# A graph network on one core: rounds of 13 groups, two tiles of each round fetched row by row, node relus on VectorE

## The chip, the cores and the metric

The kernel runs on one core of a Trainium2 chip. The metric is the device time of one execution in microseconds (us). The kernel before takes 6143.23 us (median of 3 runs, 6143.08 to 6143.71).

## What is computed

A three-layer message-passing network over 12,500 nodes and 212,500 edges, all in float32 with 128 features. `x`, the indices and the weights are inputs; the edges come sorted by destination.

```python
h = relu(layernorm(x))                      # 12500 x 128
h = h @ enc_w + enc_b;  h_list = [h]
for l in range(3):
    e   = edge_attr @ edge_w[l] + edge_b[l]            # 212500 x 16 -> x 128
    msg = relu(h_list[l][src] + e)                     # rows gathered by source node
    agg = segment_sum(msg, dst)                        # summed by destination node
    z   = (1 + eps[l]) * h_list[l] + agg
    z   = relu(z @ w1[l] + b1[l]) @ w2[l] + b2[l]      # 128 -> 256 -> 128
    h_list.append(relu(z))
out = x + concat(h_list) @ out_w + out_b
```

## The kernel before, in words

Edges are cut into tiles of 128 (one edge for each partition) and tiles into groups of four: 416 groups in a layer, the last of one tile. A ring of 16 slots in the SBUF tensor `rows` holds the gathered source rows, one slot for a group; a *round* is one turn of the ring, 26 rounds in a layer. The three layers run one after the other, since the rows that a layer gathers are the ones that the layer before stored.

For every group k of a round b the engines do this, each in its own program order:

- **GpSimd** (line 399) waits until the slot's last user is summed (`agg_done`, line 423) and issues one indirect DMA for each tile, which gathers 128 rows of 512 bytes. In slots 13 (`SHARED_GROUP`) and 14 (`SYNC_GROUP`) it gathers three tiles only; the fourth tile is fetched row by row, with one small DMA for each row, by other engines.
- **SyncE** (`fetch_body`, lines 339 to 349) fetches all 128 rows of the fourth tile of slot 14 and rows 0 to 47 of that of slot 13: 176 DMAs in a round (line 336). The addresses come from `row_at`, loaded into registers in chunks of 16 (line 333).
- **ScalarE** fetches rows 48 to 127 of slot 13's fourth tile, eight after each of its first ten relus of a round (`fetch_rows`, lines 568 to 574).
- **TensorE** makes the edge terms of group k + 2 (`edge_terms`, line 669), then the window sums of group k (`window_sums`, line 673), which wait for the relu of group k (line 735).
- **VectorE** builds the one-hot matrix of group k (line 914), adds the window sums of group k - 2 to the aggregate (`accumulate`, line 924; it waits for TensorE), and then adds the edge terms of group k to the gathered rows (`add_terms`, line 928), once rows and edge terms are there. At the end of a round it adds the last two window sums before it starts the next.
- **ScalarE** applies the relu to the group's rows (line 584), which releases TensorE's sums. Its program is one stream: wait for the sum of group k, relu of group k, then whatever else stands behind group k in `edge_body`: the load of the next edge attributes (line 564, behind the second group of a half), node work, and the row fetches.

So VectorE's add of group k needs the window sums of group k - 2, and these need the relu of group k - 2.

Node work is done in *units* of 512 nodes (24 in a layer and a rest of 256) inside the rounds. A round has two halves of 8 groups; a table worked out in the prologue says which unit, if any, each half carries. In the second, third and fourth group of a half TensorE runs `node_z` (lines 692, 694), `node_h` (line 700) and `node_out` (lines 710, 713). ScalarE runs `relu_z` in the third (line 526, two instructions) and `relu_h` in the fourth (line 535). VectorE runs `node_take` in the fifth (lines 965 to 971), and ScalarE stores the unit's rows in the sixth.

A prologue of some 130 us normalises x, encodes it, stores the table of layer 0 from SyncE (line 298) and prepares the indices. GpSimd's gathers of layer 0 start while its second part still runs on TensorE, ScalarE and VectorE.

Of the kernel before, what the change touches and what calls it, by code (L numbers as in the profile page):

```python
# [5 lines left out]
P = 128  # L6
# [5 lines left out]
HB = 8  # L12
RING = 16
# [8 lines left out]
SYNC_GROUP, SHARED_GROUP = 14, 13  # L22
SHARED_BY_SYNC = 48
CHUNK = 16
ACT_ROWS = 8
# [4 lines left out]
def gnn_kernel(nc, x_t, src_t, src_g, dst_t, dst_g, ea_t, enc_w, enc_b, edge_w, edge_b, w1, b1, w2, b2,  # L30
# [17 lines left out]
    NB = NGP // HB  # L48
    NBU = NG // HB
# [7 lines left out]
    assert ND * UT + LAST == -(-nodes // P) and NB == -(-NG // HB) and NGP <= P * GR and NI <= NBU  # L57
    assert REST == RING and EP % CHUNK == 0 and SHARED_BY_SYNC % CHUNK == 0
    assert (EP - SHARED_BY_SYNC) % ACT_ROWS == 0 and (EP - SHARED_BY_SYNC) // ACT_ROWS < SHARED_GROUP < SYNC_GROUP < RING - 1

# [7 lines left out]
    with ctx:  # L68
# [11 lines left out]
        rows = sb("rows", [P, RING, TG, D])  # L80
# [179 lines left out]
        def uses_of_half(half):  # L260
            return NFULL + (REST > half * HB)

# [20 lines left out]
        def _(sp):  # L283
            for part in range(2):
                load_x(sp, part)
            sp.wait_ge(s_zeroed, 4)
            sp.dma_start(attr[0][0:KA - 1, :], ea_t[:, 0:HB * EP]).then_inc(attr_in[0], 16)
            for j in range(TG):
                cols = slice(j * D, (j + 1) * D)
                sp.dma_start(edgew[j * KE:(j + 1) * KE, :, cols], edge_w.rearrange("l k n -> k l n"))\  # L290
                  .then_inc(s_edgew, 16)
                sp.dma_start(edgew[KA - 1:KA, :, cols], edge_b.rearrange("(a l) n -> a l n", a=1))\
                  .then_inc(s_edgew, 16)
            for i in range(NI):
                sp.wait_ge(p_biased, i + 1)
                made = p_rows[i % 4].rearrange("p t d -> p (t d)")
                if i < ND:
                    sp.dma_start(h_units[0][:, i, :], made).then_inc(p_stored[i % 4], 16)
                else:
                    sp.dma_start(h_last[0], made[:, 0:LAST * D]).then_inc(p_stored[i % 4], 16)  # L300
                if i == 8:
                    sp.dma_start(dst_n, dst_g.rearrange("c (g e) -> c g e", g=GR)).then_inc(s_dst, 16)
                if i == 10:
                    sp.dma_start(dst_i, dst_t).then_inc(s_dst_t, 16)
                if i == 12:
                    sp.dma_start(idx[0:EP, :], src_t).then_inc(idx_in, 16)
                    for u, k in enumerate((SYNC_GROUP, SHARED_GROUP)):
                        of_group = src_g.rearrange("(b t) e -> b t e", t=RING * TG)[:, k * TG + TG - 1, :]
                        sp.dma_start(row_at[u:u + 1, :].rearrange("a (b e) -> a b e", e=EP), of_group.unsqueeze(0))\
                          .then_inc(row_at_in, 16)  # L310
                if i == 14:
                    sp.dma_start(encb[:, :], enc_b).then_inc(s_par, 16)
                    sp.dma_start(b1s[:, :], b1).then_inc(s_par, 16)
                    sp.dma_start(b2s[:, :], b2).then_inc(s_par, 16)
                if i == 16:
                    sp.dma_start(eps1[:, 0:L], eps.partition_broadcast(P)).then_inc(s_par, 16)
                    sp.dma_start(outw[:, :, :], out_w.rearrange("(l k) n -> k l n", k=D)).then_inc(s_par, 16)
                    sp.dma_start(outb[:, :], out_b.partition_broadcast(P)).then_inc(s_par, 16)

            named = itertools.count()  # L320
            for l in range(L):
# [7 lines left out]
                def fetch_rows(b, u, group, count, fetched):  # L329
                    for first in range(0, count, CHUNK):  # L330
                        with ExitStack() as held:
                            at = [held.enter_context(sp.register(f"sync_at{next(named)}")) for _ in range(CHUNK)]
                            sp.load(at, row_at[u:u + 1, bass.ds(b * EP + first, CHUNK)])  # L333
                            for i in range(CHUNK):
                                row = rows[first + i:first + i + 1, group, TG - 1, :]
                                sp.dma_start(row.bitcast(u8), table_row(l, sp, at[i])).then_inc(fetched, 16)  # L336
# [23 lines left out]
                fetch_body(NFULL)  # L360
# [7 lines left out]
        def _(g):  # L368
# [34 lines left out]
            for l in range(L):  # L403
# [12 lines left out]
                for group in range(NG):  # L416
# [3 lines left out]
                    if l == 0 and group == HB:  # L420
                        g.wait_ge(s_ready, 1)
# [12 lines left out]
        def _(act):  # L434
            for s in (hid_ready, h_ready):
                act.sem_inc(s, N0)
# [82 lines left out]
            for l in range(L):  # L519
                load_weights(l)  # L520

                def relu_z(i, cols=UC):
                    n = i + l * NU
                    for c, ps in enumerate((zh_ps, zt_ps)):
                        wait_apart(act, z_done, n * HC + (c + 1 + N0))
                        nc.scalar.activation(hid[:, c, 0:cols], ps[:, 0:cols], ACT.Relu,  # L526
                                             bias=b1s[:, l * HC + c:l * HC + c + 1])\
                          .then_inc(hid_ready, 1)

                def relu_h(i, cols=UC):  # L530
                    n = i + l * NU
                    act.wait_ge(h_done, n + (1 + N0))
                    act.wait_ge(o_done, n + N0)
                    wait_apart(act, seeded, (L - 1) * NU + N0 if l == L - 1 else n + N0)
                    nc.scalar.activation(h_t[:, 0:cols], zh_ps[:, 0:cols], ACT.Relu, bias=b2s[:, l:l + 1])\  # L535
                      .then_inc(h_ready, 1)

# [16 lines left out]
                def node_body(i):  # L554
                    relu_z(i)
                    relu_h(i)
                    (store if l < L - 1 else store_out)(i)

                def load_next_attr(b, half):
# [3 lines left out]
                    else:  # L563
                        act.dma_start(attr[1 - half][0:KA - 1, :],
                                      ea_t[:, bass.ds((b * 2 + half + 1) * (HB * EP), HB * EP)])\
# [10 lines left out]
                def edge_body(b, groups):  # L576
                    for k in range(groups):
                        half, kk = k // HB, k % HB
                        if kk == 0 and groups - k >= HB:
# [22 lines left out]
                nodes_left(act, first, node_body)  # L602
                relu_z(ND, LAST * P)
                relu_h(ND, LAST * P)
# [5 lines left out]
        def _(pe):  # L610
# [67 lines left out]
            for l in range(L):  # L678
# [45 lines left out]
                def edge_body(b, groups):  # L724
                    first_group = b * RING + l * NG

                    def e_terms(k):
                        half, kk = k // HB, k % HB
# [11 lines left out]
                    for k in range(groups):  # L740
                        half, kk = k // HB, k % HB
                        if kk == 0 and groups - k >= HB:
# [4 lines left out]
                        if kk in (1, 2, 3) and groups - half * HB >= HB:  # L747
                            with pe.If(unit > 0):
                                if kk == 1:
                                    wait_apart(pe, added, first_group + (half * HB + S0))  # L750
# [21 lines left out]
        def _(dve):  # L772
            dve.sem_inc(summed, S0)
            dve.sem_inc(added, S0)
            for s in (seeded, rows_ready, o_added):
# [50 lines left out]
            def find_units():  # L826
# [7 lines left out]
                own(v.tensor_reduce(later_lo[cur][:, 0:NB], base_row[:, :].rearrange("a (b g) -> a b g", g=HB), AX.X,  # L834
                                    ALU.min))
# [121 lines left out]
            for l in range(L):  # L957
                dve.wait_ge(seeded, l * NU + N0)

                def node_take(i, tiles=UT):  # L960
# [13 lines left out]
                def edge_body(b, groups):  # L974
# [8 lines left out]
                    for k in range(groups):  # L983
                        half, kk = k // HB, k % HB
                        if kk == 0:
                            if groups - k >= HB:
                                unit = load_unit(dve, b * 2 + half)
                            dve.load(bases[half * HB:(half + 1) * HB], base_row[0:1, bass.ds(b * RING + half * HB, HB)])
# [4 lines left out]
                        by_rows = {SYNC_GROUP: sync_fetched, SHARED_GROUP: shared_fetched}  # L993
# [5 lines left out]
                        dve.wait_ge(gathered[k], (b + (l * uses_of_slot(k) + 1)) * (16 * (TG - (k in by_rows))))  # L999
# [12 lines left out]
                nodes_left(dve, first, node_take)  # L1012
# [63 lines left out]
```

## Time and profile before

| | us |
|---|---|
| median of the runs | 6143.23 |
| the profiled execution | 6140.5 |
| its span, first to last instruction | 6138.7 |
| GpSimd busy | 4595.5 (75%) |
| TensorE busy (matmul) | 4785.9 (78%) |
| VectorE busy | 1656.2 (27%) |
| ScalarE busy | 985.9 (16%) |
| mean granted TensorE clock | 0.581 of 2.4 GHz |

Busy time counts the engines' data instructions. Loads into registers and the issuing of DMAs take time on an engine's sequencer and count as idle there, so SyncE is not in the table at all, though it issues 13,728 row DMAs, and ScalarE, which issues 6,240, looks idler than it is. In the timeline such work stands under `SPq` and `ACTq`. A gather on GpSimd is a row `DMA_INDIRECT`; the idle time in brackets behind it is the time since the one before.

### The profile page before, as it was taken

How to read it: one execution, taken by the hardware profiler on the slowest of the kernel's cores; microseconds unless marked ns; L12 is line 12 of the kernel's file. 1: busy time of each engine (PE TensorE's matmuls, PEld its weight loads, DVE VectorE, ACT ScalarE, POOL GpSimd, SP SyncE). 2: the span in 40 equal slices, each digit the busy share in tenths (PEclk: the TensorE clock that was granted, in tenths of full speed). 3: DMA queues.
4: the chain of work that ended last, by engine and by line, in shares of the span. 5: the costliest groups of instructions: out<-in, count | busy, mean ns of one | idle time of the engine just before them, and what ended most of it. 6: DMA issues, size and time to landing. Idle time of an engine off the chain costs nothing.

```text
span 6138.7 us, 99522 instructions
## 1 busy us (share of the span) xinstructions
PE 4785.9 (78%) x14396; PEld 2978.1 (49%) x14397; DVE 1656.2 (27%) x4182; ACT 985.9 (16%) x1583; POOL 4595.5 (75%) x4920
## 2 busy tenths in 40 slices
PE   7877777777777777777777778777777777777777
PEld 5544444444444444444444444444444444444444
DVE  6222222222222222222222222222222222222222
ACT  4111111111111111111111111111111111111111
POOL 6777777777777677777777777767777777777776
PEclk8555555555555555555555555555555555555555
DMA  4222222222222222222222222222222222222222
GB/s 141 65 65 65 65 65 65 65 65 63 65 65 65 64 64 64 66 65 66 66 66 66 64 66 66 66 63 64 65 65 65 63 65 65 65 65 64 65 65 60
DMA packets 226648, 409.09 MB, mean 67 GB/s; under 512 B 102529, under 2 KB 125444, under 8 KB 225460
## 3 DMA queue, kind: packets, MB, share of 16 engines
q0 software_dynamic: 154464, 316.65, 19.8%
q10 hardware_dynamic: 38032, 69.39, 3.9%
q1 hardware_dynamic: 33579, 18.23, 1.0%
q14 instruction: 557, 4.55, 0.2%
q8 instruction: 16, 0.26, 0.0%
HBM read 378.17 MB, written 25.69 MB: 66 GB/s over the span
## 4 chain that ended last, share of the span: by engine, by line
POOL 32%; PE 17%; issue 16%; SPq 15%; DMA 11%; DVE 4%; ACT 3%; ACTq 1%; DVEq 0%; POOLq 0%
POOL rows L399 32%; SPq L336 12%; DMA rows<-h_table,idx 11%; PE bank L673 11%; PE bank L669 5%; SPq L333 3%; DVE rows L928 3%; ACT rows L584 3%; ACTq L574 1%; PE bank L692 0%; PE bank L647 0%; PE bank L694 0%; PE bank L639 0%; PE bank L632 0%; DVE onehot L790 0%
## 5 line engine op out<-in xcount | busy, mean ns | idle before, releaser
L399 POOL DMA_INDIRECT rows<-h_table,idx x4827 | 4558.6, 944 | 1505.4 <-issue 1335.1
L673 PEld LDWEIGHTS bank<-onehot,rows 128*128 128x128 f32 x9966 | 2066.9, 304 | 2718.0 <-ACT rows L584 2607.6
L673 PE MATMUL bank<-onehot,rows 128*128 128x64 f32 x9966 | 2212.9, 397 | 1300.8 <-ACT rows L584 1295.4
L669 PE MATMUL bank<-edgew,attr 65*128 65x512 f32 x2496 | 2216.2, 1000 | 9.3 <-DMA w2s<-w 9.3
L928 DVE TENSOR_TENSOR rows<-bank,rows 128x512 f32<-128x512 f32 x1248 | 860.9, 690 | 3470.0 <-DMA rows<-h_table,idx 3128.0
L584 ACT ACTIVATE rows<-rows 128x512 f32<-128x512 f32 x1248 | 783.5, 628 | 5048.0 <-DVE rows L928 4837.8
L669 PEld LDWEIGHTS bank<-edgew,attr 65*128 65x128 f32 x2496 | 657.9, 307 | 269.3 <-issue 269.3
L914 DVE TENSOR_TENSOR onehot<-bank,dst_rel 128x256 f32<-128x256 f32 x1248 | 518.7, 416 | 204.7 <-issue 204.7
L924 DVE TENSOR_TENSOR agg_t<-bank,agg_t 128x64 f32 x1248 | 271.7, 218 | 696.5 <-PE bank L673 691.5
L692 PE MATMUL bank<-agg_t,w1s 128*128 (+1 forms) x150 | 149.1, 1097 | 1.5 <-DVE agg_t L924 1.5
L713 PE MATMUL bank<-outw,h_t 128*128 128x128 f32 x588 | 149.2, 397 | 0.7 <-ACT h_t L535 0.7
L700 PE MATMUL bank<-hid,w2s 128*128 128x512 f32 x300 | 145.2, 607 | 0.0
L713 PEld LDWEIGHTS bank<-outw,h_t 128*128 128x128 f32 x588 | 141.9, 325 | 1.4 <-ACT h_t L535 1.4
L694 PE MATMUL bank<-agg_t,w1s 128*128 (+1 forms) x150 | 127.8, 952 | 0.0
L526 ACT ACTIVATE hid<-bank,b1s 128x512 f32<-128x512 f32 (+1 forms) x150 | 94.5, 667 | 22.7 <-PE bank L694 12.2
L694 PEld LDWEIGHTS bank<-agg_t,w1s 128*128 128x128 f32 x150 | 50.4, 336 | 74.9 <-issue 74.4
L700 PEld LDWEIGHTS bank<-hid,w2s 128*128 128x128 f32 x300 | 52.2, 196 | 37.1 <-issue 34.4
L971 DVE TENSOR_TENSOR out_acc<-bank,out_acc 128x512 f32 (+1 forms) x75 | 50.5, 674 | 18.0 <-PE bank L713 18.0
L535 ACT ACTIVATE h_t<-bank,b2s 128x512 f32<-128x512 f32 (+1 forms) x75 | 49.8, 664 | 22.8 <-PE bank L700 22.4
L394 POOL TENSOR_SCALAR rows<-out_acc,rstd,nmr 128x128 f32<-128x128 f32 x75 | 32.3, 448 | 23.4 <-DVE nmr L806 23.4
L965 DVE COPY h_n<-bank 128x512 f32<-128x512 f32 (+1 forms) x50 | 33.7, 674 | 59.1 <-PE bank L710 59.1
L647 PEld LDWEIGHTS bank<-outw,hid 128*128 128x128 f32 x200 | 28.9, 210 | 27.9 <-issue 20.8
(83 smaller groups left out, 468.4 us busy)
## 6 DMA issues: line engine op xcount, KB each, us to landing
rows<-h_table SPq DMA_DIRECT2D x13728, 0.5 KB
rows<-h_table ACTq DMA_DIRECT2D x6240, 0.5 KB
rows<-h_table,idx POOLq DMA_INDIRECT x4827, 2.5
attr<-ea_t ACTq DMA_DIRECT2D x155, 256.0 KB
h_table<-h_n ACTq DMA_DIRECT2D x48, 256.0 KB, 2.3
h_table<-rows SPq DMA_DIRECT2D x24, 256.0 KB, 2.7
out<-out_acc ACTq DMA_DIRECT2D x24, 256.0 KB, 2.3
out_acc<-x_t ACTq DMA_DIRECT2D x4, 1280.0 KB, 16.3
```

The costliest lines, as they stand in the source:

```text
L333: sp.load(at, row_at[u:u + 1, bass.ds(b * EP + first, CHUNK)])
L336: sp.dma_start(row.bitcast(u8), table_row(l, sp, at[i])).then_inc(fetched, 16)
L399: return g.indirect_dma_start(dst, None, h_table[l % 2], bass.IndirectOffsetOnAxis(ap=index, axis=0))
L584: nc.scalar.activation(part, part, ACT.Relu).then_inc(relued, 1)
L669: return nc.tensor.matmul(dst[0:EP, 0:tiles * D], cols, edgew[:, l, 0:tiles * D], start=True, stop=True)
L673: last = nc.tensor.matmul(dst[:, 0:WIN], rows[0:EP, slot, j, :], onehot[0:EP, hot_slot, j, :], start=(j == 0), stop=(j == tiles - 1))
L694: nc.tensor.matmul(zt_ps[:, 0:cols], w1s[:, D:2 * D], moving, start=True, stop=True).then_inc(z_done, 1)
L700: last = nc.tensor.matmul(zh_ps[:, 0:cols], w2s[:, c, :], hid[:, c, 0:cols], start=(c == 0), stop=(c == HC - 1))
L713: last = nc.tensor.matmul(zh_ps[:, j * D:(j + 1) * D], cols[:, j, :], outw[:, l + 1, :], start=True, stop=True)
L914: return v.tensor_tensor(onehot[0:EP, slot, 0:tiles, :], numbers[0:EP, :].unsqueeze(1).broadcast_to([EP, tiles, WIN]), dst_rel[0:EP, bass. ...
L924: return v.tensor_tensor(cols, ps[:, 0:WIN], cols, ALU.add)
L928: return v.tensor_tensor(part, ps[0:EP, 0:tiles * D].rearrange("p (t d) -> p t d", d=D), part, ALU.add)
```

## The change

- A round has 13 groups instead of 16 (`RING`), and a layer 32 rounds instead of 26. `rows` keeps its 16 slots (`SLOTS`) for the prologue's use, but the ring turns over 13 of them.
- The halves of a round have 7 and 6 groups.
- The slots whose fourth tile is fetched by rows are 10 and 11. In the last round of a layer nothing is fetched by rows; GpSimd gathers all four tiles there.
- SyncE fetches 128 + 16 rows in a round instead of 128 + 48, with register loads of 32 addresses instead of 16.
- ScalarE fetches 112 rows in a round instead of 80: 28 rows at a time (`ACT_ROWS`), behind groups 0, 2, 4 and 6 (`ACT_EVERY`), instead of 8 rows behind each of groups 0 to 9.
- `relu_z` and `relu_h` of the nodes run on VectorE (as `tensor_scalar` with add and max), in the third and fourth group of a half, in front of `node_take` in the fifth.
- In the prologue the loads of the first edge attributes and of the edge weights, which stood ahead of SyncE's first store, stand behind stores 18 and 19 to 22 of 25.

The core of the diff:

```diff
-HB = 8
-RING = 16
+HALVES = ((0, 7), (7, 6))
+HB = 7
+RING = 13
+SLOTS = 16
-SYNC_GROUP, SHARED_GROUP = 14, 13
-SHARED_BY_SYNC = 48
-CHUNK = 16
-ACT_ROWS = 8
+SYNC_GROUP, SHARED_GROUP = 11, 10
+SHARED_BY_SYNC = 16
+CHUNK = 32
+ACT_ROWS = 28
+ACT_EVERY = 2
@@ SyncE, prologue
-            sp.wait_ge(s_zeroed, 4)
-            sp.dma_start(attr[0][0:KA - 1, :], ea_t[:, 0:HB * EP]).then_inc(attr_in[0], 16)
...
+                if i == 18:
+                    sp.wait_ge(s_zeroed, 4)
+                    sp.dma_start(attr[0][0:KA - 1, :], ea_t[:, 0:HB * EP]).then_inc(attr_in[0], 16)
+                if 0 <= i - (NI - TG - 2) < TG:
+                    j = i - (NI - TG - 2)
+                    cols = slice(j * D, (j + 1) * D)
+                    sp.dma_start(edgew[j * KE:(j + 1) * KE, :, cols], edge_w.rearrange("l k n -> k l n"))\
+                      .then_inc(s_edgew, 16)
...
@@ SyncE, layers
-                fetch_body(NFULL)
@@ GpSimd
-                    if slot in (SYNC_GROUP, SHARED_GROUP):
+                    if slot in (SYNC_GROUP, SHARED_GROUP) and group < NFULL * RING:
                         tiles = TG - 1
@@ ScalarE, edge_body: behind the relu of group k
-                        if kk in (2, 3, 5) and groups - half * HB >= HB:
+                        if kk == 5:
                             with act.If(unit > 0):
-                                (relu_z if kk == 2 else relu_h if kk == 3 else
-                                 store if l < L - 1 else store_out)(unit_before(unit))
-                        if k == 0 and not (isinstance(b, int) and b == 0 and l == 0):
-                            wait_apart(act, agg_done, b * RING + (l * NG + SHARED_GROUP + 1 + S0 - RING))
-                        if k < (EP - SHARED_BY_SYNC) // ACT_ROWS:
-                            fetch_rows(b, SHARED_BY_SYNC + k * ACT_ROWS)
+                                (store if l < L - 1 else store_out)(unit_before(unit))
+                        if not isinstance(b, int):
+                            if k == 0:
+                                wait_apart(act, agg_done, b * RING + (l * NG + SHARED_GROUP + 1 + S0 - RING))
+                            if k % ACT_EVERY == 0 and k // ACT_EVERY < (EP - SHARED_BY_SYNC) // ACT_ROWS:
+                                fetch_rows(b, SHARED_BY_SYNC + k // ACT_EVERY * ACT_ROWS)
@@ VectorE
+                def relu_z(i, cols=UC):
+                    n = l * NU + i
+                    for c, ps in enumerate((zh_ps, zt_ps)):
+                        dve.wait_ge(z_done, n * HC + (c + 1 + N0))
+                        v.tensor_scalar(hid[:, c, 0:cols], ps[:, 0:cols], b1s[:, l * HC + c:l * HC + c + 1], 0.0,
+                                        ALU.add, ALU.max).then_inc(hid_ready, 1)
@@ VectorE, edge_body: behind add_terms of group k
-                        if kk == 4 and groups - half * HB >= HB:
+                        if kk in (2, 3, 4):
                             with dve.If(unit > 0):
-                                node_take(unit_before(unit))
+                                (relu_z, relu_h, node_take)[kk - 2](unit_before(unit))
```

## Rows read from the trace of the kernel before

**Rows 1.** The page's head: span, and busy time of each engine.
```profile
span 6138.7 us, 99522 instructions
PE 4785.9 (78%) x14396; PEld 2978.1 (49%) x14397; DVE 1656.2 (27%) x4182; ACT 985.9 (16%) x1583; POOL 4595.5 (75%) x4920
```
**Rows 2.** The gathers' line: count, duration (min/median/max ns), first and last start.
```profile
L399 POOL DMA_INDIRECT rows<-h_table,idx x4827: 940/944/3425, 66.8 to 6124.1; - x194
```
**Rows 3.** The view of waits: who waited for whom, us, times, longest.
```profile
POOL rows L399 <- PE bank L673: 164.6, 539, 0.3
...
DVE rows L928 <- DMA rows<-h_table: 237.2, 25, 16.9
```
**Rows 4.** Timeline of ScalarE, layer 0's first round: start, duration, what, idle before.
```profile
132.98 0.63 ACT L584 ACTIVATE rows<-rows 128x512 f32<-128x512 f32 x1 [5.99 <-DVE rows L928]
...
149.47 0.63 ACT L584 ACTIVATE rows<-rows 128x512 f32<-128x512 f32 x1 [3.16 <-DVE rows L928]
150.38 2.68 ACTq L574 DMA_DIRECT2D rows<-h_table  x8
153.17 0.63 ACT L584 ACTIVATE rows<-rows 128x512 f32<-128x512 f32 x1 [3.06 <-DVE rows L928]
...
160.86 0.63 ACT L584 ACTIVATE rows<-rows 128x512 f32<-128x512 f32 x1 [3.27 <-DVE rows L928]
...
165.34 0.63 ACT L584 ACTIVATE rows<-rows 128x512 f32<-128x512 f32 x1 [3.85 <-DVE rows L928]
```
**Rows 5.** The same timeline further on, groups 10 to 15 and the next round's first.
```profile
173.22 1.15 ACT L584 ACTIVATE rows<-rows 128x512 f32<-128x512 f32 x2 [3.80 <-DVE rows L928]
176.91 0.63 ACT L584 ACTIVATE rows<-rows 128x512 f32<-128x512 f32 x1 [2.54 <-DVE rows L928]
180.56 0.63 ACT L584 ACTIVATE rows<-rows 128x512 f32<-128x512 f32 x1 [3.02 <-DVE rows L928]
183.89 0.63 ACT L584 ACTIVATE rows<-rows 128x512 f32<-128x512 f32 x1 [2.70 <-DVE rows L928]
187.15 0.63 ACT L584 ACTIVATE rows<-rows 128x512 f32<-128x512 f32 x1 [2.63 <-DVE rows L928]
193.04 0.63 ACT L584 ACTIVATE rows<-rows 128x512 f32<-128x512 f32 x1 [5.25 <-DVE rows L928]
```
**Rows 6.** Timeline of SyncE's queue, around the register load between two chunks.
```profile
3006.08 1.87 SPq L336 DMA_DIRECT2D rows<-h_table  x2
3007.68 5.03 SPq L336 DMA_DIRECT2D rows<-h_table  x16
```
**Rows 7.** Engines' busy time in two stretches, with the granted clock as PEclk.
```profile
core 0: us, PE busy (x) PEld busy (x) DVE busy (x) ACT busy (x) POOL busy (x), PEclk, DMA share, GB/s
147.00:225.00 78.00, 75.86 (x209) 46.95 (x208) 25.61 (x63) 12.98 (x21) 58.79 (x64) 0.50 0.24 61
2600.00:2677.40 77.40, 60.21 (x181) 36.92 (x181) 20.26 (x51) 11.80 (x19) 58.50 (x63) 0.59 0.25 65
```
**Rows 8.** Timeline of TensorE where a node unit's first matmuls stand.
```profile
303.10 2.02 PE L669 MATMUL bank<-edgew,attr 65*128 65x512 f32 x2
...
306.63 2.02 PE L692 MATMUL bank<-agg_t,w1s 128*128 x2
...
310.52 1.00 PE L673 MATMUL bank<-onehot,rows 128*128 128x64 f32 x8
```
**Rows 9.** Timeline across the seam from layer 0 to layer 1.
```profile
2078.76 0.94 POOL L399 DMA_INDIRECT rows<-h_table,idx  x1 [0.30 <-issue]
...
2082.51 0.31 ACT L584 ACTIVATE rows<-rows 128x128 f32<-128x128 f32 x1 [1.00 <-DVE rows L928]
...
2092.60 0.94 POOL L399 DMA_INDIRECT rows<-h_table,idx  x1 [12.89 <-issue]
...
2099.63 0.63 ACT L584 ACTIVATE rows<-rows 128x512 f32<-128x512 f32 x1 [11.01 <-DVE rows L928]
```
**Rows 10.** Timeline at the end: the last relu on edge rows.
```profile
6128.09 0.31 ACT L584 ACTIVATE rows<-rows 128x128 f32<-128x128 f32 x1 [0.82 <-DVE rows L928]
```
**Rows 11.** VectorE's scaling from SBUF to SBUF in `node_take`: count, duration, first and last.
```profile
L967 DVE TENSOR_SCALAR agg_t<-h_t,eps x50: 344/477/683, 240.6 to 4113.2; 128x512 f32 x48, 128x256 f32<-128x256 f32 x2
```

More of the change, by code:

```diff
@@ L47, in gnn_kernel @@
     NGP = NTE // TG
-    NB = NGP // HB
-    NBU = NG // HB
+    NB = NGP // RING * 2
+    NBU = NB
     L = w1.shape[0]
@@ L79, in gnn_kernel @@
         agg_t = sb("agg_t", [P, NP + WIN])
-        rows = sb("rows", [P, RING, TG, D])
+        rows = sb("rows", [P, SLOTS, TG, D])
         attr = [sb(f"attr{i}", [KA, HB * EP]) for i in range(2)]
@@ L260, in uses_of_half, with in_half @@
         def uses_of_half(half):
-            return NFULL + (REST > half * HB)
+            return NFULL + (REST > HALVES[half][0])
+        def in_half(k):
+            half = int(k >= HALVES[1][0])
+            return half, k - HALVES[half][0]
         def load_left(eng):
@@ L330, in fetch_rows @@
                     for first in range(0, count, CHUNK):
+                        here = min(CHUNK, count - first)
                         with ExitStack() as held:
-                            at = [held.enter_context(sp.register(f"sync_at{next(named)}")) for _ in range(CHUNK)]
-                            sp.load(at, row_at[u:u + 1, bass.ds(b * EP + first, CHUNK)])
-                            for i in range(CHUNK):
+                            at = [held.enter_context(sp.register(f"sync_at{next(named)}")) for _ in range(here)]
+                            sp.load(at, row_at[u:u + 1, bass.ds(b * EP + first, here)])
+                            for i in range(here):
                                 row = rows[first + i:first + i + 1, group, TG - 1, :]
@@ L419, in _ @@
                         g.wait_ge(idx_in, 16)
-                    if l == 0 and group == HB:
+                    if l == 0 and group == 8:
                         g.wait_ge(s_ready, 1)
@@ L520, in _ @@
                 load_weights(l)
[L522 to L536, printed above, removed]
                 def store_out(i):
@@ L563, in load_next_attr @@
                     else:
-                        act.dma_start(attr[1 - half][0:KA - 1, :],
-                                      ea_t[:, bass.ds((b * 2 + half + 1) * (HB * EP), HB * EP)])\
+                        start, n = HALVES[1 - half]
+                        cols = bass.ds((b + half) * (RING * EP) + start * EP, n * EP)
+                        act.dma_start(attr[1 - half][0:KA - 1, 0:n * EP], ea_t[:, cols])\
                            .then_inc(attr_in[1 - half], 16)
@@ L577, in edge_body @@
                     for k in range(groups):
-                        half, kk = k // HB, k % HB
-                        if kk == 0 and groups - k >= HB:
+                        half, kk = in_half(k)
+                        if kk == 5:
                             unit = load_unit(act, b * 2 + half)
@@ L601, in _ @@
                 far_passes(act, n_far, far_pass)
-                nodes_left(act, first, node_body)
-                relu_z(ND, LAST * P)
-                relu_h(ND, LAST * P)
+                nodes_left(act, first, store if l < L - 1 else store_out)
                 if l < L - 1:
@@ L727, in e_terms @@
                     def e_terms(k):
-                        half, kk = k // HB, k % HB
+                        half, kk = in_half(k)
                         if kk == 0:
@@ L740, in edge_body @@
                     for k in range(groups):
-                        half, kk = k // HB, k % HB
-                        if kk == 0 and groups - k >= HB:
+                        half, kk = in_half(k)
+                        if kk == 0:
                             unit = load_unit(pe, b * 2 + half)
@@ L746, in edge_body @@
                         sums(k)
-                        if kk in (1, 2, 3) and groups - half * HB >= HB:
+                        if kk in (1, 2, 3):
                             with pe.If(unit > 0):
                                 if kk == 1:
-                                    wait_apart(pe, added, first_group + (half * HB + S0))
+                                    wait_apart(pe, added, first_group + (HALVES[half][0] + S0))
                                     node_z(unit_before(unit))
@@ L774, in _ @@
             dve.sem_inc(added, S0)
-            for s in (seeded, rows_ready, o_added):
+            for s in (seeded, rows_ready, o_added, hid_ready, h_ready):
                 dve.sem_inc(s, N0)
@@ L833, in find_units @@
                 cur = 0
-                own(v.tensor_reduce(later_lo[cur][:, 0:NB], base_row[:, :].rearrange("a (b g) -> a b g", g=HB), AX.X,
-                                    ALU.min))
+                in_rounds = base_row[:, :].rearrange("a (b r) -> a b r", r=RING)
+                low = later_lo[cur][:, 0:NB].rearrange("a (b h) -> a b h", h=2)
+                for half, (start, n) in enumerate(HALVES):
+                    own(v.tensor_reduce(low[:, :, half], in_rounds[:, :, start:start + n], AX.X, ALU.min))
                 reach = 1
@@ L958, in _, with relu_h, node_body @@
                 dve.wait_ge(seeded, l * NU + N0)
+                def relu_z(i, cols=UC):
[4 more added lines that the diff above has]
+                                        ALU.add, ALU.max).then_inc(hid_ready, 1)
+                def relu_h(i, cols=UC):
+                    n = l * NU + i
+                    dve.wait_ge(h_done, n + (1 + N0))
+                    dve.wait_ge(o_done, n + N0)
+                    dve.wait_ge(seeded, (L - 1) * NU + N0 if l == L - 1 else n + N0)
+                    v.tensor_scalar(h_t[:, 0:cols], zh_ps[:, 0:cols], b2s[:, l:l + 1], 0.0, ALU.add, ALU.max)\
+                     .then_inc(h_ready, 1)
+                def node_body(i):
+                    relu_z(i)
+                    relu_h(i)
+                    node_take(i)
                 def node_take(i, tiles=UT):
@@ L983, in edge_body @@
                     for k in range(groups):
-                        half, kk = k // HB, k % HB
+                        half, kk = in_half(k)
                         if kk == 0:
-                            if groups - k >= HB:
-                                unit = load_unit(dve, b * 2 + half)
-                            dve.load(bases[half * HB:(half + 1) * HB], base_row[0:1, bass.ds(b * RING + half * HB, HB)])
+                            unit = load_unit(dve, b * 2 + half)
+                            dve.load(bases[k:k + HALVES[half][1]], base_row[0:1, bass.ds(b * RING + k, HALVES[half][1])])
                         tiles = real_tiles(b, k)
```

33 lines of the change are left out of this document (14 added, 19 removed).

## The prediction

> **What bounds the kernel now.** I read the page's busy times first [rows 1], then the line of the costliest group, the gathers [rows 2], then the waits. Busy shares mislead here: GpSimd shows 75%, but it issued 4827 gathers from 66.8 to 6124.1 us. Take off the two seams between layers (the first one keeps it idle from 2078.76 to 2092.60 [rows 9], the second some 2 us longer) and a gather is left every 1.25 us for the whole span. Its waits for a free slot were never longer than 0.3 us [rows 3], which is the ordinary space between two gathers. So GpSimd sets the pace: 62 gathers in a round, 77.5 us. TensorE comes second: 60.2 busy us in 77.4 [rows 7]. The reader should see two things beside this. First, nobody else's chain is far away: in layer 0, where the first relu on edges comes only at 132.98 us [rows 4] while the gathers have run since 66.8, the rest of the engines work off a backlog, and that stretch shows what their chain can do when the data is there. Second, ScalarE's 16% hides its DMA issues.
>
> **The gathers.** Two by-row tiles in 31 rounds instead of 26 make 62 instead of 52 tiles a layer that GpSimd doesn't gather, so 30 gathers fewer over three layers: 30 x 1.25 = 37.5 us off, if GpSimd still sets the pace. A round of 13 groups is then 50 gathers, 62.5 us. That is the time every other chain has to meet.
>
> **SyncE.** 16 rows in a chunk take 5.03 us, and from the row at 3006.08 with one more behind the load to the end there were 1.87 us [rows 6]: about 0.32 us a row and 1.3 us for a load of 16 addresses. After: 144 x 0.32 = 46 us and five loads of, I take it, 1.5 to 2.3 us, 54 to 58 us in a round of 62.5. It had 176 x 0.32 + 11 x 1.3 = 71 of 77.5. It keeps up in both, though its 128 rows must follow the sums of group 11 one round before; I give it no price.
>
> **ScalarE, the term that decides.** [rows 4] have the backlogged pace with 8 rows behind each relu: from a relu to the first row 0.91 us (the address load is in it), 2.68 us for the 8 rows, 0.11 to the next relu; 3.70 from relu to relu (149.47 to 153.17). That hid under the 5.0 us which four gathers take. Now 28 rows stand behind one relu. Rows: 28 x 0.32 = 9.0 us (9.7 at the 0.34 of the eight). Load and rest: no row has 28 addresses; between 1.0 (the load doesn't grow) and 2.3 (it grows per address as fast as it may from 8 to 16); I take 2.1, since the loads of 16 in [rows 6] are longer than those of 8 in [rows 4]. So 11.1 us a burst, bounds 9.9 and 12.2. In it the relu of the next, odd group can't run: two groups cost 11.1 + about 0.7, where their eight gathers bring 10.0. From the relu of group 0 to that of group 7 there are four bursts (44.4), three steps of about 0.75 to an even group (0.54 in [rows 5], more with the attribute load), and the unit number's load before group 5, 0.8 (160.86 to 165.34 against 3.7 without it [rows 4]): 47.4 us. On arrival alone it would be 35.
>
> Then the round isn't over. From group 7's relu on, the chain is the one of [rows 5]: two relus together behind the last burst (173.22), then 176.91, 180.56, 183.89, 187.15, and 193.04 for the first of the next round. TensorE paces it: edge terms and sums of a group take about 3.4 us, VectorE's add of group k waits for the sums of k - 2, and at the round's end VectorE must add the last window before it starts again. Seven relus in, five groups and the boundary on, is just what groups 7 to 12 and the next group 0 are after the change: 19.8 us. Together 67.2 us for a round, against 62.5 from GpSimd. TensorE can't work ahead during the bursts, as its sums wait for the relus that are stuck.
>
> **Nodes.** With 512 nodes a unit and 30 nodes a group, 14 units of a layer fall into second halves of the first 31 rounds, 9 into first halves, one into the last round. In a second half the unit's 8 us of TensorE work lie in the TensorE-paced part; but behind it the array runs at its upper level (a group's sums in 1.00 us, after edge terms at 2.02 us for two before it [rows 8]), which gives some back; and VectorE, not ScalarE, now waits for the z products. I take 4.5 us, between 3 and 8. In a first half there are 5 idle us of TensorE in each pair of groups: 1.3 us, between 0 and 3. A round: (14 x 4.5 + 9 x 1.3) / 31 = 2.4. ScalarE loses 225 relus of about 0.65 us, which I credit at nothing beyond this, as the bursts are what holds it.
>
> So **a round takes 69.6 us** and the chain ScalarE, TensorE, VectorE sets the pace in all 93 of them; GpSimd waits for slots instead.
>
> **The ring of 13.** With less lead GpSimd would stall in layer 0's start: 50 gathers from 66.8 end at about 132, and the first slot is free after the first sums, some 3 us behind the relu at 132.98: 4 us on GpSimd. It costs nothing where GpSimd isn't the bound.
>
> **The prologue.** The moved loads leave the first input loads alone and meet SyncE among its last stores; nine issues of about 0.6 us against a 60 us lead of the gathers over the first relu. Nothing, give or take 2 us; if the x tiles come sooner, a microsecond gained.
>
> **The sum.** First relu at 132.98 [rows 4]. 93 rounds x 69.6 = 6473. Three last rounds without bursts at 3.4 us a group and one unit: 3 x 45.5 = 136.5. Two seams from the last relu to the first gather (2082.51 to 2092.60 [rows 9]), 2 x 10.1, and from there to the relu (2099.63), 2 x 7.0. The end: 6138.7 - 6128.09 = 10.6 [rows 1, 10]. Span 6787. The profiled execution was 4.5 us of span below the median of the runs: **6792 us**, 10.6% slower.
>
> The bounds on the term that decides: with bursts of 9.9 and units at their lowest a round is 42.6 + 19.8 + 1.4 = 63.8, and the time 6253; with bursts of 12.2 and units at their highest 51.8 + 19.8 + 4.5 = 76.1 and 7397. I put the likely part of this, 6270 to 7150, as the range of the case.
>
> **A rule that speaks against this chain.** [rows 7] show TensorE busy 75.9 of 78 us at a granted clock of 0.50, the lower level of 1.2 GHz; only behind the node matmuls of [rows 8] is it at 2.4 GHz. I take TensorE's pace from these rows. The Trainium skill (TensorE: Matmul & The Clock Gate, Part 1) says that the clock gate opens after sustained activity; by it a TensorE that is backlogged would run near the upper level, and [rows 7] disagree.
>
> **Rivals.** *GpSimd stays the bound.* The chain from group 7 on is faster than [rows 5] (TensorE at the upper level, about 2 us a group, which makes the 19.8 some 14), or bursts overlap with relus in a way I don't see. Then 6143.2 - 37.5 + 4 for the shorter ring = 6110. For it: the total of ScalarE's work, 4 x 11.1 + 13 x 0.7 = 54 us, does fit in 62.5; against it: it isn't spread, and [rows 4, 5] are the same instructions in the same order. 12%. *Just at the edge*, a round of 62.5 to 63: 6150, 3%. *GpSimd is the bound but is held up by VectorE.* 225 node relus come to VectorE at about 0.68 us. If each kept a gather from being issued, up to 153 us: 6110 + 153 = 6263. Against it: VectorE's scaling from SBUF to SBUF, 50 times [rows 11], left gathers at 1.25 us. The Trainium skill (SBUF — State Buffer, Who interferes with whom) says that VectorE in a two-port mode and GpSimd shut each other out for a whole instruction; [rows 11] don't show it as a cost. The decisive point is whether GpSimd's rows near such relus show more than 0.3 us between gathers. 3%. *SyncE becomes the bound*: 58 us plus the landing and the sums of group 11, near 62.5; it decides only if a round were under 63, so it is inside the first rival.
>
> **Chances.** The forecast's chain 82%, GpSimd bound 12%, edge 3%, lock-out 3%. 0.2% is about what a measurement of this kernel can tell from no change. Faster 0.13, same 0.02, slower 0.85. The range 6270 to 7150 leaves out the first rival and the tails.
>
> **What would show it.** Right: GpSimd's waits for TensorE's sums (line 399 behind `window_sums`) rise from 165 us to hundreds, in all three layers; ScalarE's timeline has `ACTq` blocks of 28 rows of about 9 us with one relu, then two relus together; relu of group 0 to group 7 about 47 us, to the next group 0 about 67 to 75. VectorE's wait for row DMAs falls away. Wrong: gathers at 1.25 us without a stall past layer 0's first round, or relus between the rows of a block; or bursts under 9.9 us.

## The result, and the profile after

The changed kernel takes 6851.86 us (median of 4 runs, 6846.06 to 6853.34), the kernel before beside it 6143.47: a ratio of 1.115, 95% interval 1.113 to 1.117. The prediction was 6792 us in a range of 6270 to 7150, slower.

The page's head and the two lines of its chain of work that ended last (shares of the span by engine, then by line):

```profile
span 6844.3 us, 106750 instructions
PE 4772.2 (70%) x14396; PEld 3103.4 (45%) x14397; DVE 1846.6 (27%) x4408; ACT 828.4 (12%) x1358; POOL 4567.8 (67%) x4890
...
ACTq 51%; PE 26%; issue 15%; DVEq 3%; DVE 3%; ACT 2%; DMA 0%; POOL 0%; SPq 0%
ACTq L561 41%; PE bank L658 13%; ACTq L558 8%; PE bank L654 8%; ACT rows L571 2%; DVEq L994 2%; DVE rows L915 1%; PE bank L698 1%; PE bank L685 1%; PE bank L677 1%; ACTq L251 1%; PE bank L679 1%; ACTq L552 1%; DVEq L251 1%; PE bank L632 0%
```

ScalarE's busy time fell to 828 us, against 986 in [rows 1], and yet half of the chain is now on its queue: line 561 issues the single rows, line 558 loads their addresses. GpSimd is out of it. The same line of the page before had GpSimd (POOL) at a third:

```profile
POOL 32%; PE 17%; issue 16%; SPq 15%; DMA 11%; DVE 4%; ACT 3%; ACTq 1%; DVEq 0%; POOLq 0%
```

The waits after say the same (who waited for whom, us, times, longest):

```profile
ACT rows L571 <- issue: 3826.7, 417, 11.8
DVE agg_t L911 <- PE bank L658: 3562.8, 982, 10.5
...
POOL rows L408 <- PE bank L658: 758.8, 392, 6.8
```

The last line answers to the first of [rows 3]: GpSimd waits up to 6.8 us for a slot where it never waited over 0.3, 759 us in all against 165. Its 4797 gathers still stand 1.25 us apart when nothing holds them. "issue" in the first line is ScalarE's own issuing: its relus wait for the engine itself.

One round of the changed kernel on ScalarE's timeline (start, duration, what, idle before):

```profile
3017.62 0.63 ACT L571 ACTIVATE rows<-rows 128x512 f32<-128x512 f32 x1 [6.20 <-DVE rows L915]
3019.72 8.97 ACTq L561 DMA_DIRECT2D rows<-h_table  x28
3028.80 0.63 ACT L571 ACTIVATE rows<-rows 128x512 f32<-128x512 f32 x1 [10.54 <-issue]
...
3029.55 0.63 ACT L571 ACTIVATE rows<-rows 128x512 f32<-128x512 f32 x1
3031.73 9.06 ACTq L561 DMA_DIRECT2D rows<-h_table  x28
3040.90 1.15 ACT L571 ACTIVATE rows<-rows 128x512 f32<-128x512 f32 x2 [10.72 <-issue]
3043.08 8.95 ACTq L561 DMA_DIRECT2D rows<-h_table  x28
3052.98 1.15 ACT L571 ACTIVATE rows<-rows 128x512 f32<-128x512 f32 x2 [10.93 <-issue]
3055.19 9.03 ACTq L561 DMA_DIRECT2D rows<-h_table  x28
3064.33 0.63 ACT L571 ACTIVATE rows<-rows 128x512 f32<-128x512 f32 x1 [10.21 <-issue]
...
3089.79 0.63 ACT L571 ACTIVATE rows<-rows 128x512 f32<-128x512 f32 x1 [6.25 <-DVE rows L915]
```

Four blocks of 28 rows, 9 us each, with two relus behind each of the first three; 46.7 us from the relu of group 0 to that of group 7, and 25.5 more to the next group 0 at 3089.79 (this round has a node unit in its second half).

From the start times of all relus on edge rows (line 571) I worked out how long the rounds take, in 93 rounds: 24 without a node unit 68.1 us, 39 with one in the second half 72.7, 30 with one in the first half 69.1; **70.3 us in the mean**, against the 77.5 that GpSimd's 62 gathers take for 16 groups before. That is 5.41 us a group, and 4.84 before.

GpSimd's stall sets in late, because its lead has to be used up first. In layer 1 the relu of a round's first group stood 0, 7, 18, 25, 31, 37, 48 and 53 us later, from round to round, than the arrival of its rows allowed; from there on it stayed at 52 to 61 us, near the 62.5 us that gathers for a full ring of 13 take. Layer 2 did the same, a little later. In layer 0 it is there from the start.

### The profile page after: what moved, and what is told of

Same layout as the page of the kernel before. It is cut to its first block, busy times and chain, and to the rows that moved or that the text cites. A ratio compares the mean times of both kernels' runs of the same rounds, so it can differ in the third digit from the quotient of the medians.

```text
span 6844.3 us, 106750 instructions
## 1 busy us (share of the span) xinstructions
PE 4772.2 (70%) x14396; PEld 3103.4 (45%) x14397; DVE 1846.6 (27%) x4408; ACT 828.4 (12%) x1358; POOL 4567.8 (67%) x4890
## 4 chain that ended last, share of the span: by engine, by line
ACTq 51%; PE 26%; issue 15%; DVEq 3%; DVE 3%; ACT 2%; DMA 0%; POOL 0%; SPq 0%
ACTq L561 41%; PE bank L658 13%; ACTq L558 8%; PE bank L654 8%; ACT rows L571 2%; DVEq L994 2%; DVE rows L915 1%; PE bank L698 1%; PE bank L685 1%; PE bank L677 1%; ACTq L251 1%; PE bank L679 1%; ACTq L552 1%; DVEq L251 1%; PE bank L632 0%
## 5 line engine op out<-in xcount | busy, mean ns | idle before, releaser
L658 PEld LDWEIGHTS bank<-onehot,rows 128*128 128x128 f32 x9966 | 2157.2, 310 | 3257.9 <-ACT rows L571 2695.3
L658 PE MATMUL bank<-onehot,rows 128*128 128x64 f32 x9966 | 2169.4, 394 | 2018.2 <-ACT rows L571 2015.0
L654 PE MATMUL bank<-edgew,attr 65*128 65x512 f32 x2496 | 2320.3, 1047 | 8.5 <-DMA w2s<-w 8.5
L571 ACT ACTIVATE rows<-rows 128x512 f32<-128x512 f32 x1248 | 757.0, 625 | 5950.0 <-issue 3826.7
L654 PEld LDWEIGHTS bank<-edgew,attr 65*128 65x128 f32 x2496 | 692.5, 321 | 307.5 <-issue 307.5
L951 DVE TENSOR_SCALAR hid<-bank,b1s 128x512 f32<-128x512 f32 (+1 forms) x150 | 110.7, 740 | 593.4 <-PE bank L677 537.0
L959 DVE TENSOR_SCALAR h_t<-bank,b2s 128x512 f32<-128x512 f32 (+1 forms) x75 | 55.5, 740 | 156.0 <-PE bank L685 156.0
```

What stands on the lines that cost most here:

```text
L571: nc.scalar.activation(part, part, ACT.Relu).then_inc(relued, 1)
L654: return nc.tensor.matmul(dst[0:EP, 0:tiles * D], cols, edgew[:, l, 0:tiles * D], start=True, stop=True)
L658: last = nc.tensor.matmul(dst[:, 0:WIN], rows[0:EP, slot, j, :], onehot[0:EP, hot_slot, j, :], start=(j == 0), stop=(j == tiles - 1))
```

## The experiments

All kernels are edits of the changed kernel. Ratios are to the kernel before, run in between on the same chip.

**The bursts.** If the row fetches on ScalarE's queue and what TensorE has left behind them set the round, two bursts fewer must give the time back, with the ring of 13 and the relus on VectorE still there. This kernel leaves out 56 of the 128 rows of the shared tile, so it computes something else; its time is what counts here.

```diff
+ACT_BURSTS = 2
...
-                            if k % ACT_EVERY == 0 and k // ACT_EVERY < (EP - SHARED_BY_SYNC) // ACT_ROWS:
+                            if k % ACT_EVERY == 0 and k // ACT_EVERY < ACT_BURSTS:
...
+                own(v.memset(rows[:, SHARED_GROUP, TG - 1, :], 0.0))
...
-                            take(dve, by_rows[k], 16 * EP)
+                            take(dve, by_rows[k], 16 * (EP if k == SYNC_GROUP else SHARED_BY_SYNC + ACT_BURSTS * ACT_ROWS))
```

> The changed kernel with two bursts of 28 row fetches on ScalarE instead of four; 56 rows of the shared tile are left out (what stands in those partitions of the buffer is used instead), everything else stays: ring of 13, node relus on VectorE, 50 gathers a round. Theory (ScalarE's bursts and TensorE behind them set a round): group 0 to 3 takes 24 us, from there to the next group 0 about 34 us, 58 and some 2 for nodes, under the 62.5 us of the gathers; GpSimd is the bound again at 1.25 us a gather: 6100 to 6140 us. Rival 'the ring of 13 starves GpSimd': stays near 6850. Rival 'VectorE's node relus': at least 6650.

Measured first: 9330 us, and 9367 for the kernel before beside it. This was on a chip on which the queues of SyncE and ScalarE issue slowly; it is told further down. The four kernels timed there say nothing on the theories, and each was timed on another chip too.

> The same kernel as e_2bursts, again, because in that call every kernel, the one before too, took 8.4 to 9.4 ms, with 0.7 us between many of SyncE's instructions. If SyncE issues a row every 0.32 us again: theory (bursts, then TensorE) 58 us of chain and 2 of nodes under the gathers' 62.5, so 6100 to 6140 us; the ring of 13 or VectorE's relus as the cause would leave it near 6850 or 6650. 56 rows of the shared tile are left out.

Measured: **6114.45 us**, ratio 0.996 (0.994 to 0.997). The waits:

```profile
POOL rows L409 <- issue: 1412.5, 4626, 0.3
POOL rows L409 <- PE bank L659: 64.5, 168, 7.0
```

GpSimd is the bound again. The median is 25 us below the kernel before beside it (6139.68), where 30 gathers fewer would give 37.5. In the profiled run a gather stood 1.2514 us behind the one before, against 1.2489, which makes 12 us over all of them; it isn't VectorE's relus, as the gathers took 944 ns in the median in the kernel with three bursts, which has them too, and 947 in the first run of the one with the relus on ScalarE. The shorter ring cost three stalls of 4.1, 6.7 and 2.5 us in layer 0's start, and none after. A round took 62.2 us in the mean.

Three bursts, with the same edit and `ACT_BURSTS = 3` (28 rows are left out):

> The changed kernel with three bursts of 28 rows instead of four; 28 rows of the shared tile are left out. Theory: group 0 to group 5 takes 35.9 us, from there 28 us to the next group 0, with nodes 66 us a round; 304 us outside the rounds: 6440 us, between 6380 and 6500. Not proportional to the bursts: the fourth costs 400 us, the third some 330, the second nothing. Rivals (ring, VectorE's relus): near 6850.

On the slow chip: 9115 us, before 9367. Again:

> The same kernel as e_3bursts (three bursts of 28 rows, 28 rows of the shared tile left out), with rows at 0.32 us again. Theory: group 0 to group 5 36.0 us, from there 0.54 + 3.15 + 3.4 + 3.4 + 3.4 + 3.3 + 3.3 + 6.8 = 27.3 to the next group 0, 63.3 us and 2.3 for nodes, 65.6 a round; 304 + 93 x 65.6 = 6405 us, between 6350 and 6450. If the time followed the number of rows, halfway between two bursts (6114) and four (6852): 6480.

Measured: **6388.54 us**, ratio 1.040 (1.038 to 1.041). A round took 65.6 us, the 65.6 that had been worked out. Two, three and four bursts give 62.2, 65.6 and 70.3 us: with two a round is the gathers' own, the third costs 3.4, the fourth 4.7. Only what goes beyond GpSimd's 62.5 us shows. In proportion to the rows it would have been 6480 us; the measured time stands 16 us below the 6405 of the forecast.

**The size of a burst or their sum.** The same 112 rows, spread:

```diff
-ACT_ROWS = 28
-ACT_EVERY = 2
+ACT_ROWS = 16
+ACT_EVERY = 1
```

> The changed kernel with the same 112 rows on ScalarE, as 16 rows behind each of groups 0 to 6 instead of 28 behind 0, 2, 4 and 6. Theory 'ScalarE's total before group 7 counts': 7 x 6.8 us + 1.5 us for the attribute and unit loads = 49 us, then 20 us: a round near 70 to 71, 6850 to 6930 us. Rival 'the size of a burst counts' (TensorE works between smaller bursts, so that nothing is left to catch up): below 6300.

On the slow chip: 8421 us, before 9367. Again:

> The same kernel as e_16x7, again. With rows at 0.32 us: theory 'ScalarE's total ahead of group 7 counts' 70 to 71 us a round, 6850 to 6930 us; rival 'the size of a burst counts' below 6300.

Measured: **7030.86 us**, ratio 1.145 (1.143 to 1.147), 100 us above the upper end of what was expected, and slower than 28 at a time. ScalarE's timeline:

```profile
3031.89 0.63 ACT L571 ACTIVATE rows<-rows 128x512 f32<-128x512 f32 x1 [6.98 <-issue]
3033.26 5.17 ACTq L561 DMA_DIRECT2D rows<-h_table  x16
3038.55 0.63 ACT L571 ACTIVATE rows<-rows 128x512 f32<-128x512 f32 x1 [6.03 <-issue]
```

6.7 to 6.8 us a step, and 7.6 at the two with another load beside it; 49 to 50 us to group 7, then the same 21: 70.1 us in a round without a unit, 72.4 in the mean. The sum ahead of group 7 counts, not its pieces; and smaller pieces have more address loads (1.4 us from relu to first row, seven times, against 2.1 four times). What the expectation missed are the units' 2.3 us a round, which it left out of its 70 to 71.

**The node relus.** Back on ScalarE, at their old places (`relu_z` and `relu_h` move with them; the unit's number is loaded at a half's first group instead of its sixth):

```diff
@@ ScalarE
-                        if kk == 5:
+                        if kk == 0:
                             unit = load_unit(act, b * 2 + half)
...
-                        if kk == 5:
+                        if kk in (2, 3, 5):
                             with act.If(unit > 0):
-                                (store if l < L - 1 else store_out)(unit_before(unit))
+                                (relu_z if kk == 2 else relu_h if kk == 3 else
+                                 store if l < L - 1 else store_out)(unit_before(unit))
@@ VectorE
-                        if kk in (2, 3, 4):
+                        if kk == 4:
                             with dve.If(unit > 0):
-                                (relu_z, relu_h, node_take)[kk - 2](unit_before(unit))
+                                node_take(unit_before(unit))
```

> The changed kernel with the node relus back on ScalarE, where they were before. Theory: they stand in the bursts' part of first halves and cost 2 us more there, and about the same in second halves: 6850 to 6950 us. Rival 'VectorE's relus, which make it wait for TensorE, are the cost': down to about 6650 us.

On the slow chip: 9438 us, before 9367. Again:

> The same kernel as e_act_relus (node relus back on ScalarE), with rows at 0.32 us again. Theory: 2 us more in rounds with a unit in the first half, the same in the others: 6850 to 6950 us. Rival 'VectorE's relus are the cost': down to about 6650 us.

Measured: **7079.54 us**, ratio 1.152 (1.151 to 1.154): worse than with them on VectorE, by 228 us, and 130 us above the range. The timeline of a round with a unit in its first half:

```profile
3033.87 0.63 ACT L592 ACTIVATE rows<-rows 128x512 f32<-128x512 f32 x1 [10.58 <-issue]
...
3034.66 0.63 ACT L592 ACTIVATE rows<-rows 128x512 f32<-128x512 f32 x1 [0.16 <-issue]
3038.47 0.69 ACT L533 ACTIVATE hid<-bank,b1s 128x512 f32<-128x512 f32 x1 [3.18 <-PE bank L701]
3040.18 0.69 ACT L533 ACTIVATE hid<-bank,b1s 128x512 f32<-128x512 f32 x1 [1.02 <-PE bank L703]
3042.26 9.43 ACTq L582 DMA_DIRECT2D rows<-h_table  x28
```

Group 1's relu was held until 3033.87 by the burst ahead, so TensorE's z products come only after it, and ScalarE stands at `relu_z` with its next burst behind it: 5 us lost. Rounds with a unit in the first half took 75.0 us, 6.0 more than with the relus on VectorE; those with one in the second half 73.1 against 72.7, those without 68.5 against 68.1. Over 93 rounds this is the 207 us between the two profiled spans. So this part of the change is worth some 200 to 230 us beside the bursts. Taking 225 relus off ScalarE had been credited at nothing, which was right for the 0.65 us of each and would have been wrong for their waits.

**The prologue.** The loads at their old place:

> The changed kernel with the loads of the first edge attributes and edge weights at their old place, ahead of SyncE's first store. Both theories: within 0.2% of the changed kernel's 6852 us; the first relu on edges at 133 to 135 us as in both traces.

The edit puts the load of `attr[0]` and the eight of `edgew` ahead of SyncE's first store again. Measured, in one run: 6842.65 us, 0.13% under 6851.86 and 3.4 us under the profiled run of the changed kernel. The first relu came at 137.6 us, outside the 133 to 135 expected, against 134.8; the last rounds made up for it (42.2 us in the mean, against 43.0), and a round took 70.28 us, against 70.32. So this part moves the first relu by 3 us and the whole by nothing that one run can show.

**A version that could keep GpSimd the bound.** All rows fetched, 100 of them on ScalarE, ten at a time:

```diff
-SHARED_BY_SYNC = 16
+SHARED_BY_SYNC = 28
...
-ACT_ROWS = 28
-ACT_EVERY = 2
+ACT_ROWS = 10
+ACT_EVERY = 1
```

> The changed kernel with 100 rows on ScalarE, 10 behind each of groups 0 to 9, and 28 + 128 on SyncE: all rows are fetched. Theory: a step with 10 rows is about 4.5 us (3.8 with 8, 6.8 with 16), under the 5.0 us of four gathers, and only three groups are left behind the last one: 45 + 2.5 + 0.5 + 3.2 + 6.8 = 58 us; SyncE needs 56 + 12 x 0.36 = 60 us. Both are under the gathers' 62.5: GpSimd is the bound, 6105 to 6135 us, 0.2 to 0.6% under the kernel before. Rival 'no margin is left' (SyncE's 60 us and the wait for its rows, or units on top): 6200 or more.

Measured: **6923.13 us**, ratio 1.127 (1.125 to 1.128). The 6105 to 6135 expected are badly missed, and the timeline shows where:

```profile
3031.89 0.63 ACT L571 ACTIVATE rows<-rows 128x512 f32<-128x512 f32 x1 [6.33 <-issue]
3033.23 3.33 ACTq L561 DMA_DIRECT2D rows<-h_table  x10
3036.67 0.63 ACT L571 ACTIVATE rows<-rows 128x512 f32<-128x512 f32 x1 [4.15 <-issue]
3039.29 3.31 ACTq L561 DMA_DIRECT2D rows<-h_table  x10
...
3073.22 3.45 ACTq L561 DMA_DIRECT2D rows<-h_table  x10
3079.58 0.63 ACT L571 ACTIVATE rows<-rows 128x512 f32<-128x512 f32 x1 [8.29 <-DVE rows L915]
```

From a relu to the first row it is 1.34 us at one step and 2.62 at the next, in turn. The trace's records of the address load have 1.0 to 1.4 us for the loads that begin at index 28, 48, 68, 88 and 108, and 2.2 to 2.6 us for 38, 58, 78, 98 and 118. These are loads of the same size in the same run, so where a load begins is what differs. The other part is the end: group 10 needs its last rows, which are issued just ahead of it (8.1 us from relu to relu in the median). To tell the two apart, the same rows in loads that all begin at a multiple of four and hold a multiple of four:

```diff
-ACT_ROWS = 10
+ACT_ROWS = [12, 8] * 5
```

(`fetch_rows` takes its count from this list.)

> As e_10x10 (100 rows on ScalarE behind groups 0 to 9, 28 + 128 on SyncE, all rows fetched), but 12 and 8 rows in turn instead of 10 each, so that every load of addresses into registers begins at a multiple of four. In e_10x10 the loads of 10 addresses took 1.0 to 1.2 us where their first index was a multiple of four (28, 48, 68, 88, 108) and 2.2 to 2.6 us where it was not (38, 58, ...). Theory (that alignment made e_10x10 slow): loads of 12 near 1.1 us, of 8 near 0.7; group 0 to 9 43 us, 6 to group 10 (its rows must land), 10.5 to the next group 0, 59.5 and 2 for nodes: under the gathers' 62.5, so 6110 to 6180 us. Rival (the wait for group 10's rows, or SyncE's 60 us, is what holds it): 6500 us or more.

Measured: **6315.62 us**, ratio 1.028 (1.027 to 1.030). 608 us came back. The loads of 12 took 0.80 to 1.15 us, those of 8 0.56 to 0.91: the ten loads of a round together 8.5 us, against 17.9. It isn't the whole: a round took 64.5 us, and GpSimd still waited.

```profile
DVE rows L915 <- DMA rows<-h_table: 952.0, 181, 9.9
...
POOL rows L408 <- PE bank L658: 141.6, 187, 4.7
```

VectorE now waits for single rows 181 times: 93 times at group 10, 697 us, and 88 times at group 11, 255 us, whose 128 rows SyncE brings. SyncE has 156 rows in a round here, and waits for a freed slot only 25 times, 76 us in all. Against the expectation, group 0 to 9 took 44.3 us instead of 43, from there to group 10 6.9 instead of 6, and from there to the next group 0 12.8 instead of 10.5 (medians of the steps). Which part of the last is SyncE's rows and which VectorE's own loads, no run tells apart. No version that was tried beats the kernel before with all rows fetched.

## Why the prediction was right, point by point

- **Who sets the pace.** ScalarE's bursts with TensorE and VectorE behind them: shown, by the chain, by GpSimd's waits, and by 6114 us without two of the bursts.
- **A burst.** Put at 11.1 us: measured 11.3 to 11.7 from the relu ahead of it to the next, 10.9 for the last. 28 rows took 9.1 in the median, 9.0 predicted; from the relu to the first row 2.1 us, as taken. For this no row had a price, and the 2.1 was a choice between 1.0 and 2.3: that it fits to a tenth is luck in part (the load by itself took 1.75 to 1.98 us). The two bounds don't quite follow from their terms, which give 10.0 and 12.0 instead of 9.9 and 12.2. Group 0 to group 7: 47.4 predicted; 47.1 in the median of the rounds without a unit in the first half, 47.7 over all.
- **Behind them.** 19.8 predicted after [rows 5], 20.8 measured. Group by group it is [rows 5] again (medians 0.54, 3.15, 3.67, 3.32, 3.38), but for the last step to the next round, 6.8 instead of 5.9. VectorE's timeline there:

```profile
3013.58 0.23 DVE L911 TENSOR_TENSOR agg_t<-bank,agg_t 128x64 f32 x1 [1.87 <-PE bank L658]
3016.57 0.42 DVE L901 TENSOR_TENSOR onehot<-bank,dst_rel 128x256 f32<-128x256 f32 x1 [2.76 <-issue]
```

  2.76 us of its own issuing. The load of the window bases into registers, 8 of them at a multiple of 16 before, is now one of 7 at 13 b. It took 0.60 us before and takes 1.63, but 1.05 in every fourth round, where 13 b is a multiple of four; and the last step is 6.3 us ahead of those rounds, against 6.7 to 6.9 ahead of the others. This was the step missed: with rounds of 13 groups most of these loads begin at an index that isn't a multiple of four, and they hold 7 and 6 values instead of 8.
- **Nodes.** 4.5 us in second halves, measured 4.6; 1.3 in first halves, measured 1.0. There were 39 and 30 such rounds, not 42 and 27.
- **Outside the rounds.** The last rounds, a layer's rest of 13 groups, took 43 us each, not 45.5; the first relu came at 134.8, not 133.0; the seams 15.6, not 17.1. 304 us together, 314 predicted.
- **The sum.** A round 70.3 instead of 69.6: 93 x 0.7 = 65 us more, 10 less outside, and the median stands 7.6 us above the profiled span instead of 4.5: 6852 instead of 6792.
- **The gathers.** 30 fewer, still 1.25 us apart. The kernel with two bursts is the first rival made true: it gave 6114, the rival's price was 6110. The ring of 13 cost it 13 us in layer 0's start, where 4 were taken.
- **SyncE.** Its loads of 32 addresses took 2.0 us, inside the 1.5 to 2.3 taken, and it kept up: it waited for freed slots 90 times, 995 us in all. That rival fell, but for the slow chip told of below.
- **The lock-out rival fell.** Gathers took 944 ns in the median before and after. The 244 that ran beside one of VectorE's 225 relus took at most 953 ns. The Trainium skill (SBUF — State Buffer, Who interferes with whom) would have the two shut each other out in a two-port mode; nothing here shows that for relus that read PSUM. It does show, small, for the 50 scalings from SBUF to SBUF, and so also in the kernel before, where the prediction read [rows 11] as showing nothing: 6 of the 51 gathers beside them took 1013 to 1167 ns, and [rows 11] has scalings of up to 683 ns where the median is 477. After 140 us no other gather of that run took over 975 ns. The changed kernel has the same (a scaling, and the gather that started in it):

```profile
4278.20 0.48 DVE L974 TENSOR_SCALAR agg_t<-h_t,eps 128x512 f32 x1
4278.33 1.17 POOL L408 DMA_INDIRECT rows<-h_table,idx  x1 [0.30 <-issue]
```

  All of it together is 1 us in 6140, so the rival's price stays at nothing.
- **The clock.** The chain's TensorE ran at a granted 0.50, 1.2 GHz, from 147 to 225 us, with 53.4 busy us of 78 (the row has PE, PEld, DVE, ACT and POOL, then the granted clock). From 140 us on it was at the upper level in a tenth of the time, each time behind node products; the rows of before at either level carried over.

```profile
147.00:225.00 78.00, 53.39 (x150) 34.74 (x150) 18.20 (x45) 8.84 (x15) 52.64 (x56) 0.50 0.22 57
```

## What to carry to other kernels

An engine's queue that issues DMAs is as busy as its issuing, whatever its busy share says: count its rows, loads and relus as one stream, and ask what is left to do for the others once a block of it ends. That the total fits into the period (the forecast's 54 us in 62.5) is not enough, as the work of the engines behind the block can't begin until it is over; the sum of the block and of what must follow it is what has to fit. And an engine may be relieved of little work and of a long wait at once: 225 short relus were worth some 200 to 230 us for where they stood.

## What the runs showed that had not been expected

**Loads of several registers depend on the index at which they begin, and on how many they are.** With 10 addresses 1.0 to 1.4 us from a multiple of four and 2.2 to 2.6 from elsewhere; 7 bases 1.05 and 1.63; 6 bases 0.83 and 1.41. With all begun at multiples of four: 8 in 0.72, 12 in 0.96, 16 in 1.2, 28 in 1.9, 32 in 2.0 us (medians). So even from a multiple of four 7 bases took longer than 8 (1.05 and 0.60, both on VectorE) and 10 addresses longer than 12 (1.17 and 0.96, both on ScalarE): what isn't a multiple of four in number costs too.

**One chip issued far slower.** The kernels timed first took 8421 to 9438 us there, and the kernel before 9367. Gathers took 943 to 946 ns in the mean there, too. The queues of SyncE and of ScalarE were the difference. SyncE's in 12 us, in the kernel with two bursts, there and on another chip:

```profile
3000.02 12.20 SPq L347 DMA_DIRECT2D rows<-h_table  x23
```

```profile
2999.90 12.03 SPq L347 DMA_DIRECT2D rows<-h_table  x31
```

On the slow chip 25 to 31% of its rows stood 0.7 us or longer behind the row before, 2.1 at the 95th percentile, where on another chip it was 3.5%; the median was 0.32 on both, as its instructions came in steps of 0.7 us in stretches only. ScalarE's bursts did the same. One of the kernel with the node relus on ScalarE, on the slow chip:

```profile
3004.34 14.51 ACTq L582 DMA_DIRECT2D rows<-h_table  x28
```

Its bursts of 28 rows took 14.2 us in the median there, against 9.1. In the kernel with two bursts SyncE's queue was 59% of the chain; in the one with the relus on ScalarE, ScalarE's was 32% and SyncE's 15%. Whether it is the supply of instructions, and why only there, was not tried and stays open. A kernel that leaves 256 row issues a round to two queues stakes its time on that.
